# Experts by choice: five tiles ahead, late sums in a row, second weights behind the gates

## Chip, cores and metric

The kernel runs on one core of one Trainium2 chip. The metric is the device time of one execution in microseconds; before the change it is 3304.93 (median of 3 runs, 3302.91 to 3306.12).

## The reference, cut to what matters

The program is a graph attention layer with its own feed-forward part, followed by a layer of experts. Only the experts are touched:

```python
# x: 4096 tokens of 512 (normalized), 8 experts, hidden width 256, top 2
logits = xf @ router_w
gate_vals, idx = jax.lax.top_k(logits, K)
gates = jax.nn.softmax(gate_vals, axis=-1)
out = jnp.zeros_like(xf)
for e in range(E):
    h = jax.nn.relu(xf @ w1[e] + b1[e]) @ w2[e] + b2[e]
    y = _layernorm(xf + h, gamma[e], beta[e])
    w = jnp.sum(jnp.where(idx == e, gates, 0.0), axis=-1)
    out = out + w[:, None] * y
return out.reshape(B, S, D)
# and around it: x = x + experts(layernorm(x))
```

## The kernel before, in words

The stage `experts` (L1792) computes each token for its two chosen experts only. It has three phases.

Routing: the 32 tiles of 128 normalized tokens are loaded (L1948), transposed by PE and copied by ACT (`z_cols`), multiplied with the router, and DVE picks the best and the second-best expert per token. It computes the two gates of each token; ACT's queue stores them into the last two columns of the rows in HBM (`z3`, called `t_z` in the profile, L2049), 4096 pieces of 8 bytes. Semaphore `s_gate_home` tells of its landing.

Listing: DVE and PE sort the tokens by expert into slots of 128 tokens. `EACH = 39` slots hold the first choices (32 full tiles and up to 7 for the remainders of 8 experts), 39 more the second ones: 78 slots, each of one expert. The list of the first choices raises `s_ready` to 1 (L2212), the list of the second ones to 2.

Slots: for slot n, POOL gathers 128 rows by an indirect DMA into `rows_sb[n % 8]` (L1995). A row of a first choice comes from `z3` and has two halves: the row's running sum (514 numbers, `PART`), and the normalized row with its two gates. PE transposes (L2274), multiplies with the expert's w1 (`up`, L2332), transposes the hidden tile (L2340) and multiplies with w2 (`down`, L2351, with b2 in front, L2346). ACT copies the transposed rows (L2059), the hidden tile (L2064), applies relu and b1 (L2070), takes the root (L2099), and multiplies beta by the gate (`outer`, L2076). DVE adds down and rows (`y`, L2220), takes the statistics (L2222, L2224), adds the base (`add_base`, L2230), applies gamma (L2237) and adds up the slot before (`outer`, L2246), which raises `e_done`. Then POOL scatters: a first choice into `summed` (`t_summed`, whole rows, L2015), a second one into the output (L2012). A slot of the second choices reads its rows from `summed`, so all scatters of the first ones must have landed.

To let PE go on over that border, the first `LATE_PARTS = 5` slots of the second choices (39 to 43) are gathered in two pieces: the normalized half from `z3` early (L1989), the sum's half from `summed` late (`late_part`, L2003 to L2007, L2005 in the profile), with a semaphore for each (`moved_part`). DVE needs the late half in `add_base` only (L2228), and does that after `gain` in these slots. `all_put` (L1998) waits for the last four scatters of the first choices.

The order on each engine is written out by hand, and each queue is in order. POOL's loop (L2022) does, in iteration n, the gather of slot n + `LEAD`, then the scatter of slot n - 1 (which waits for `e_done`), then in iterations 39 to 43 the late part of slot n. A gather waits for its buffer: `e_done` of slot n - 8 and, for a first choice, the landing of its scatter (L1983 to L1985). PE's loop (L2363) does, in iteration n: the transpose of slot n + 2, up of n + 1, down of n, the transpose of the hidden tile of n + 1. ACT's loop (L2088) does the columns of n + 2, the hidden copies of n + 1, the root of n and outer of n + 1; ahead of the loop stands slot 0's outer, behind a wait for beta (L2085). DVE waits for gamma ahead of its first slot (L2250). PE waits for w1 ahead of the first up and for b2 and w2 ahead of its loop (L2361, L2362).

SP's queue (L1940) issues the weights after the last routing tile: b2's parts to HBM, b1, w1, w2, b2 back, gamma, beta. w1 and w2 have 4096 KB each, gamma and beta, copied to all partitions, 2048 KB each.

Of the kernel before, what the change touches and what calls it, by code (L numbers as in the profile page):

```python
# [10 lines left out]
P = 128  # L11
# [14 lines left out]
VROW = HEADS * VHEAD  # L26
PART = C + 2
WITH_SUM = 2 * PART
LATE_PARTS = 5
BOTH = C + VROW  # L30
MERGED = (3, 11, 19, 27)
DVE_HEADS = (HEADS - 1, HEADS - 2)
# [1759 lines left out]
def experts(nc, moved, moved_part, count, z3, router, w1, b1, w2, b2, gamma, beta, summed, b2_home, out):  # L1792
# [15 lines left out]
    EACH = T + E - 1  # L1808
    SLOTS = TOP * EACH
    TURN = 8  # L1810
    LEAD = 4
    Y = 4
    HALF = 4
    LIST_TURNS = 4
# [2 lines left out]
    with ExitStack() as ctx:  # L1817
        def sb(name, shape, dt=F32):
            return ctx.enter_context(nc.sbuf_tensor("m_" + name, shape, dt))

        def ps(name, shape, dt=F32):
            return ctx.enter_context(nc.psum_tensor("m_" + name, shape, dt))
# [3 lines left out]
        def sem(name):  # L1826
            used.append(ctx.enter_context(nc.semaphore("ms_" + name)))
            return used[-1]

        w1_sb, w2_sb = sb("w1", [P, E, KC, F]), sb("w2", [P, E, FC, C])  # L1830
# [48 lines left out]
        put_at = sb("put_at", [P, SLOTS], I32)  # L1879
        part_of = sb("part_of", [P, 2, LATE_PARTS], I32)  # L1880
        turned = [ps(f"turned{b}", [P, C]) for b in range(2)]
# [9 lines left out]
        s_w1, s_w2, s_b2, s_gamma, s_beta = (sem(n) for n in ("w1", "w2", "b2", "gamma", "beta"))  # L1891
        s_b2_rows, s_b2_cut, s_b2_home = sem("b2_rows"), sem("b2_cut"), sem("b2_home")
        s_c, s_cut, s_dve, s_low, s_ratio = (sem(n) for n in ("c", "cut", "dve", "low", "ratio"))
        s_counted, s_listed, s_ready, s_gate, s_gate_home = (sem(n) for n in ("counted", "listed_all", "ready", "gate", "gate_home"))
# [18 lines left out]
        def tile_rows(a, i, per, u):  # L1913
            v = a.rearrange("(n p) c -> n p c", p=P)
            return v[bass.ds(i * per + u, 1), :, :].rearrange("a p c -> (a p) c")
# [4 lines left out]
        def flat(x):  # L1920
            return x.rearrange("p a c -> p (a c)")

        def second(n):
            return n >= EACH

        def late(n):
            return EACH <= n < EACH + LATE_PARTS

# [3 lines left out]
        def wait_put(eng, n):  # L1932
            eng.wait_ge(put[n % Y], count + 16 * (n // Y + 1))
# [5 lines left out]
        @block.sync  # L1939
        def _(eng):  # L1940
            eng.dma_start(router_sb[:, :, :], router.rearrange("(k p) e -> p k e", p=P)).then_inc(s_c, 16)
            eng.dma_start(b2_rows[:, :], b2).then_inc(s_b2_rows, 16)
            z_of = z3[:, PART:PART + C]
            for i in range(T // TURN):
                for u in range(TURN):
                    if i:
                        r_turn.wait(eng, i - 1, u)
                    eng.dma_start(z_rows[:, u, :], tile_rows(z_of, i, TURN, u)).then_inc(r_load.sem(u), 16)  # L1948
            eng.wait_ge(s_b2_cut, 3 * PARTS - 4)
            eng.dma_start(b2_home, b2_parts[:, :, :]).then_inc(s_b2_home, 16)  # L1950
            eng.dma_start(b1_sb[:, :, :], b1).then_inc(s_w1, 16)
            eng.dma_start(w1_sb[:, :, :, :], w1.rearrange("e (k p) f -> p e k f", p=P)).then_inc(s_w1, 16)
            eng.dma_start(w2_sb[:, :, :, :], w2.rearrange("e (k p) c -> p e k c", p=P)).then_inc(s_w2, 16)
            eng.wait_ge(s_b2_home, 16)
            eng.dma_start(b2_sb[:, :, :], b2_home.rearrange("e k c -> k e c")).then_inc(s_b2, 16)
            for dst, a, landed in ((gamma_sb, gamma, s_gamma), (beta_sb, beta, s_beta)):
                eng.dma_start(flat(dst[:, :, :]), a.rearrange("e c -> (e c)").partition_broadcast(P)).then_inc(landed, 16)

        @block.gpsimd
        def _(eng):  # L1960
            for a, value in ((ones, 1.0), (zeros, 0.0), (eps, EPS), (ones_b, 1.0)):
                eng.memset(a[:, :], value).then_inc(s_cut, 1)
            eng.memset(go_on[:, :, :], 1.0).then_inc(s_cut, 1)
            eng.memset(go_on_e[:, :, :], 1.0).then_inc(s_cut, 1)
            for a, step, n, down, first_one in ((falling, -1, E, 0, E), (row_id, 0, 1, 1, 1), (slot_at, 1, EACH, 0, 0),
                                                (turn_b, 1, T, 0, 0)):
                eng.iota(a[:, :], pattern=[[step, n]], base=first_one, channel_multiplier=down,
                         allow_small_or_imprecise_dtypes=True).then_inc(s_cut, 1)
            eng.iota(iota_2[:, :, :], pattern=[[1, P], [0, 2]], base=0, channel_multiplier=0,
                     allow_small_or_imprecise_dtypes=True).then_inc(s_cut, 1)  # L1970
            eng.wait_ge(s_cut, 11)
            eng.memset(go_on[:, :, 0:1], 0.0).then_inc(s_cut, 1)
            eng.memset(go_on_e[:, :, 0:1], 0.0).then_inc(s_cut, 1)
            for m, of, op, other in ((ident, ones, ALU.is_equal, 0.0), (not_after, zeros, ALU.is_gt, -1.0)):
                eng.affine_select(out=m[:, :], in_=of[:, :], compare_op=op, fill=other, base=0,
                                  pattern=[[1, P]], channel_multiplier=-1).then_inc(s_cut, 1)

            z3_parts, summed_parts = (a.rearrange("n (h w) -> (n h) w", h=2) for a in (z3, summed))

            def gather(n):  # L1980
                u = n % TURN
                if n >= TURN:
                    e_done.wait(eng, 0, n - TURN)  # L1983
                    if not second(n - TURN):
                        wait_put(eng, n - TURN)  # L1985
                if late(n):
                    if n == EACH:
                        eng.wait_ge(s_ready, 2)
                    eng.indirect_dma_start(rows_sb[:, u, PART:], None, z3_parts,  # L1989
                                           bass.IndirectOffsetOnAxis(part_of[:, 1, n - EACH:n - EACH + 1], 0)  # L1990
                                           ).then_inc(got[u], 16)
                else:
                    if second(n):
                        all_put(n)
                    eng.indirect_dma_start(rows_sb[:, u, :], None, summed if second(n) else z3,  # L1995
                                           bass.IndirectOffsetOnAxis(row_of[:, n:n + 1], 0)).then_inc(got[u], 16)

            def all_put(n):  # L1998
                if n <= EACH + LATE_PARTS:
                    for k in range(EACH - Y, EACH):  # L2000
                        wait_put(eng, k)

            def late_part(n):  # L2003
                all_put(n)
                eng.indirect_dma_start(rows_sb[:, n % TURN, 0:PART], None, summed_parts,  # L2005
                                       bass.IndirectOffsetOnAxis(part_of[:, 0, n - EACH:n - EACH + 1], 0)
                                       ).then_inc(moved_part[n - EACH], 16)  # L2007

            def scatter(n):
                e_done.wait(eng, 0, n)  # L2010
                if second(n):
                    eng.indirect_dma_start(out, bass.IndirectOffsetOnAxis(put_at[:, n:n + 1], 0), y[:, n % Y, :], None,  # L2012
                                           bounds_check=NODES - 1, oob_is_err=False).then_inc(put[n % Y], 16)
                else:
                    eng.indirect_dma_start(summed, bass.IndirectOffsetOnAxis(put_at[:, n:n + 1], 0), rows_sb[:, n % TURN, :], None,  # L2015
                                           bounds_check=NODES - 1, oob_is_err=False).then_inc(put[n % Y], 16)

            eng.wait_ge(s_ready, 1)
            eng.wait_ge(s_gate_home, 16)
            for n in range(LEAD):  # L2020
                gather(n)
            for n in range(SLOTS):  # L2022
                if n + LEAD < SLOTS:
                    gather(n + LEAD)
                if n:
                    scatter(n - 1)
                if late(n):
                    late_part(n)
            scatter(SLOTS - 1)
            for n in range(SLOTS - Y, SLOTS):  # L2030
                wait_put(eng, n)
# [72 lines left out]
        def _(eng):  # L2104
# [69 lines left out]
            for c in range(TOP):  # L2174
# [33 lines left out]
                if c == 1:  # L2208
                    few = token[:, c, 0:LATE_PARTS]
                    st.link(nc.vector.tensor_scalar(part_of[:, 0, :], few, 2.0, None, ALU.mult))  # L2210
# [167 lines left out]
def graph_layer(nc, a, out):  # L2378
# [5 lines left out]
    with ExitStack() as ctx:  # L2384
        moved = [ctx.enter_context(nc.semaphore(f"moved{n}")) for n in range(MOVES)]
        moved_both = [ctx.enter_context(nc.semaphore(f"moved_both{n}")) for n in range(2)]
        moved_part = [ctx.enter_context(nc.semaphore(f"moved_part{n}")) for n in range(LATE_PARTS)]
        stages(nc, a, out, moved, moved_both, moved_part, scratch)
# [58 lines left out]
```

## Time and profile before

| | |
|---|---|
| median of 3 runs | 3304.93 us |
| profiled execution | 3307.92 us |
| its span | 3306.2 us |
| PE busy | 2772.7 us (84%) |
| DVE busy | 2521.6 us (76%) |
| ACT busy | 1701.4 us (51%) |
| POOL busy | 1935.0 us (59%) |
| routing, listing and slots | 2778 to 3306 us of the span |

The span runs from the first to the last instruction. Engines are PE (TensorE), DVE (VectorE), ACT (ScalarE), POOL (GpSimd) and SP; a q behind a name is its queue. A busy PE is not PE at its peak: the ends of matmuls are modelled, and a matmul that starts late can show as a longer one. Times of day below are microseconds from the start of the span.

### The profile page before, as it was taken

The page shows a single profiled execution, that of the slowest core. Times are in us where ns is not written, and L with a number is a line of the kernel's source. Part 1 is how long each engine was busy: PE and PEld are TensorE (multiplying, and loading weights), DVE is VectorE, ACT ScalarE, POOL GpSimd, SP SyncE. Part 2 cuts the span into 40 slices and gives each one's busy share as a digit, 9 for nine tenths or more (in the row PEclk, how much of TensorE's full clock was granted, in tenths as well). Part 3 has the DMA queues.
Part 4 walks back from the last instruction along what each step waited for, and adds up shares of the span by engine and source line. Part 5 has one row for each costly group of instructions (what it writes and reads, how often), then busy time and mean ns, then how long its engine had stood idle before and what let it go on. Part 6 is the DMA issues. An engine that isn't in the chain of part 4 may idle for free. (4 is left out here: it accounts for less than half of the span.)

```text
span 3306.2 us, 51862 instructions
## 1 busy us (share of the span) xinstructions
PE 2772.7 (84%) x12057; PEld 1710.6 (52%) x12057; DVE 2521.6 (76%) x5238; ACT 1701.4 (51%) x5713; POOL 1935.0 (59%) x1959
## 2 busy tenths in 40 slices
PE   6987888780888888886999999998999997699797
PEld 6544444450333333332555655567888885355454
DVE  8776666660999999998999999996566563577576
ACT  5222222220666566555999999993443432244343
POOL 2777777776777777776777777762222221044344
PEclk9888888885999999998999999997999999899999
DMA  4554555544888888887777878774221222765343
GB/s 168 197 182 167 173 173 170 174 147 152 261 258 261 262 260 259 261 258 243 216 231 231 233 231 232 230 205 112 68 71 61 74 71 94 226 200 188 119 155 108
DMA packets 248065, 610.11 MB, mean 185 GB/s; under 512 B 60466, under 2 KB 69578, under 8 KB 243037
## 3 DMA queue, kind: packets, MB, share of 16 engines
q0 software_dynamic: 130000, 376.49, 38.2%
q1 hardware_dynamic: 113661, 230.27, 20.2%
q8 instruction: 113, 1.85, 0.2%
q14 instruction: 179, 1.47, 0.1%
q10 hardware_dynamic: 4112, 0.03, 0.1%
HBM read 488.89 MB, written 123.26 MB: 185 GB/s over the span
## 5 line engine op out<-in xcount | busy, mean ns | idle before, releaser
L1275 PE MATMUL at_pair<-wide,hot_t 128*128 x1152 | 583.2, 621 | 120.7 <-ACT hot_t L1126 106.4
L1324 PE MATMUL at_pair<-product,v_hot 128*128 128x260 f32 x2304 | 617.2, 400 | 48.7 <-DVE product L1074 21.2
L364 POOL DMA_INDIRECT records<-staged,address x544 | 545.6, 1003 | 182.5 <-issue 161.9
L914 POOL DMA_INDIRECT fetched<-t_v,at_index x504 | 487.3, 967 | 188.0 <-issue 86.6
L904 POOL DMA_INDIRECT fetched<-t_k,at_index x504 | 487.4, 967 | 154.8 <-issue 102.0
L1324 PEld LDWEIGHTS at_pair<-product,v_hot 128*128 128x128 f32 x2304 | 394.5, 190 | 266.2 <-issue 158.4
L660 PE MATMUL qkv_prod<-wide 128*128 128x512 f32 x768 | 397.5, 681 | 96.8 <-ACT wide L404 96.8
L1066 DVE TENSOR_TENSOR wide<-at_pair,wide 128x520 f32 x576 | 397.3, 690 | 14.1 <-issue 10.3
L1275 PEld LDWEIGHTS at_pair<-wide,hot_t 128*128 128x128 f32 x1152 | 186.2, 189 | 385.0 <-issue 381.8
L1134 ACT ACTIVATE product<-product 128x64 f32<-128x64 f32 x864 | 215.9, 250 | 286.3 <-DVE product L993 284.9
L993 DVE TENSOR_TENSOR product<-at_pair,fetched 128x512 f32<-128x512 f32 x504 | 342.3, 682 | 25.3 <-DMA fetched<-t_k,at_index 18.9
L947 DVE TENSOR_REDUCE raw_score<-product 128x7 f32<-128x448 f32 x576 | 329.7, 575 | 0.0
L660 PEld LDWEIGHTS qkv_prod<-wide 128*128 128x128 f32 x768 | 165.6, 220 | 304.5 <-issue 205.6
L1213 ACT ACTIVATE product<-fetched,act_weight 128x65 f32<-128x65 f32 x1008 | 288.8, 333 | 0.0
L1074 DVE TENSOR_TENSOR product<-fetched,at_turn 128x390 f32<-128x390 f32 x504 | 276.4, 549 | 2.7 <-ACT act_weight L1193 1.5
L1526 POOL TENSOR_TENSOR f_base<-f_base,wide 128x512 f32<-128x512 f32 x32 | 41.0, 1280 | 343.6 <-DVE f_rows_in L1567 343.6
L1168 ACT ACTIVATE at_shared<-iota_f,low_neg 128x128 f32<-128x128 f32 x576 | 222.7, 387 | 0.0
L1718 PE MATMUL f_up<-f_zT,f_w 128*128 128x256 f32 x1536 | 192.5, 285 | 17.5 <-ACT f_h L1674 17.5
L1207 ACT ACTIVATE v_hot<-at_shared 128x128 f32<-128x128 f32 x576 | 175.8, 305 | 45.3 <-PE at_pair L1324 42.2
L1718 PEld LDWEIGHTS f_up<-f_zT,f_w 128*128 128x128 f32 x1536 | 186.7, 192 | 20.7 <-ACT f_h L1674 20.6
L1718 PE MATMUL f_down<-f_w,f_hT 128*128 128x512 f32 x768 | 185.6, 397 | 2.3 <-issue 2.3
L392 ACT COPY staged<-bias_sb 128x128 f32<-128x128 f32 x34 | 10.1, 297 | 333.2 <-DMA records<-staged,address 332.2
(327 smaller groups left out, 4647.7 us busy)
## 6 DMA issues: line engine op xcount, KB each, us to landing
row_bc<-in_src SPq DMA_DIRECT2D x34, 1024.0 KB, 5.4
pair_rows<-kept_v SPq DMA_DIRECT2D x72, 260.0 KB, 4.2
low_bc<-low_row SPq DMA_DIRECT2D x34, 512.0 KB
wide<-in_x SPq DMA_DIRECT2D x64, 256.0 KB, 3.2
t_z<-wide SPq DMA_DIRECT2D x64, 256.0 KB, 3.1
kept_v<-pair_rows SPq DMA_DIRECT2D x36, 260.0 KB, 3.7
kept_v<-at_shared SPq DMA_DIRECT2D x36, 260.0 KB, 3.8
records<-staged,address POOLq DMA_INDIRECT x544, 2.3
```

The costliest lines, as they stand in the source:

```text
L364: eng.indirect_dma_start(records, bass.IndirectOffsetOnAxis(address[:, b, u:u + 1], 0), staged[:, b, u, :], None,).then_inc(put[b][u], 16)
L660: last = nc.tensor.matmul(prod[n][:, :], zT[:, c, kc * P:(kc + 1) * P], w[:, n, kc, :], start=(kc == 0), stop=(kc == KC - 1))
L904: eng.indirect_dma_start(fetched[:, n % SLOTS, 0:C], None, k, bass.IndirectOffsetOnAxis(index[:, t:t + 1], 0)).then_inc(s_row[n % SLOTS], 16)
L914: eng.indirect_dma_start(fetched[:, n % SLOTS, :], None, v, bass.IndirectOffsetOnAxis(index[:, t:t + 1], 0)).then_inc(s_row[n % SLOTS], 16)
L947: nc.vector.tensor_reduce(raw[:, b, u % PAIR, u // PAIR, 0:heads], product[:, u % 4, 0:heads * D].rearrange("p (h d) -> p h d", d=D), AX.X ...
L993: nc.vector.tensor_tensor(product[:, u % 4, 0:C], q_edge[u % 4], key_rows(i, u), ALU.mult).then_inc(r_product.sem(u), 1)
L1066: nc.vector.tensor_tensor(to, pair[u % 3][:, :, 0:HALF], to, ALU.add).then_inc(r_total.sem(u), 1)
L1074: nc.vector.tensor_tensor(product[:, u % 4, 0:V_DVE * VHEAD].rearrange("p (h w) -> p h w", h=V_DVE), value_rows(m, u)[:, 0:V_DVE * VHEAD]. ...
L1213: ins = nc.scalar.activation(product[:, u % 4, h * VHEAD:(h + 1) * VHEAD], value_rows(m, u)[:, h * VHEAD:(h + 1) * VHEAD], ACT.Copy, scale ...
L1275: nc.tensor.matmul(q_edge[u % 4], hot_t[:, g % 2, u % BATCH * P:(u % BATCH + 1) * P], q_sb[:, bass.ds(at, 1), :].rearrange("p a c -> p (a ...
L1324: last = nc.tensor.matmul(pair[u % 3][:, n, 0:HALF], hot[:, u % 4, :], product[:, u % 4, n * HALF:(n + 1) * HALF], start=True, stop=True)
L1718: last = nc.tensor.matmul(out, stationary(a, k), moving(b, k), start=(k == 0 and n == 0), stop=(k == chunks - 1 and n == len(PASSES) - 1))
```

## The change

Two constants go up by one, the late parts are issued together, and two groups of loads change places around a new wait: SP waits for the landing of the gates, then issues b2, w2, gamma and beta in this order.

```diff
-LATE_PARTS = 5
+LATE_PARTS = 6
...
-    LEAD = 4
+    LEAD = 5
...
             eng.dma_start(w1_sb[:, :, :, :], w1.rearrange("e (k p) f -> p e k f", p=P)).then_inc(s_w1, 16)
-            eng.dma_start(w2_sb[:, :, :, :], w2.rearrange("e (k p) c -> p e k c", p=P)).then_inc(s_w2, 16)
+            eng.wait_ge(s_gate_home, 16)
             eng.wait_ge(s_b2_home, 16)
             eng.dma_start(b2_sb[:, :, :], b2_home.rearrange("e k c -> k e c")).then_inc(s_b2, 16)
+            eng.dma_start(w2_sb[:, :, :, :], w2.rearrange("e (k p) c -> p e k c", p=P)).then_inc(s_w2, 16)
             for dst, a, landed in ((gamma_sb, gamma, s_gamma), (beta_sb, beta, s_beta)):
                 eng.dma_start(flat(dst[:, :, :]), a.rearrange("e c -> (e c)").partition_broadcast(P)).then_inc(landed, 16)
...
                 if n:
                     scatter(n - 1)
-                if late(n):
-                    late_part(n)
+                if n == EACH:
+                    for m in range(LATE_PARTS):
+                        late_part(EACH + m)
             scatter(SLOTS - 1)
```

Slot 44 now belongs to those gathered in two pieces, and the six late parts all stand in POOL's queue behind the scatter of slot 38.

## Rows read from the trace of the kernel before

**Rows 1.** Busy time by stretch: engine us (instructions), granted clock, DMA share, GB/s.
```profile
2850.00:2900.00 50.00, 30.39 (x158) 19.97 (x158) 31.32 (x93) 16.71 (x37) 9.69 (x10) 0.71 0.58 182
2900.00:2950.00 50.00, 47.05 (x187) 28.75 (x188) 35.41 (x78) 22.48 (x59) 22.26 (x20) 1.00 0.61 202
...
3200.00:3250.00 50.00, 49.60 (x199) 30.25 (x198) 37.54 (x82) 23.37 (x62) 24.46 (x21) 1.00 0.47 154
```

**Rows 2.** Timeline of POOL: start, duration, instruction, idle before and its releaser.
```profile
2893.21 1.42 POOL L2015 DMA_INDIRECT t_summed<-m_rows,m_put_at  x1 [17.57 <-DVE m_rows L2246]
...
3086.73 1.01 POOL L2015 DMA_INDIRECT t_summed<-m_rows,m_put_at  x1 [1.93 <-DVE m_rows L2246]
...
3137.19 1.38 POOL L2012 DMA_INDIRECT out<-m_y,m_put_at  x1 [1.22 <-DVE m_y L2246]
...
3286.23 1.40 POOL L2012 DMA_INDIRECT out<-m_y,m_put_at  x1 [3.68 <-DVE m_y L2246]
...
3296.53 0.98 POOL L2012 DMA_INDIRECT out<-m_y,m_put_at  x1 [0.86 <-DVE m_y L2246]
```

**Rows 3.** The chain that ended last, in order of time: start, duration, what.
```profile
2849.19 18.43 DMA t_z<-m_gate
...
2890.70 0.70 DVE m_stats L2222
...
2894.93 5.38 DMA m_rows<-t_z,m_row_of
2901.57 1.99 PE m_up L2332 x8
...
2906.44 1.73 PE m_up L2332 x8
...
2911.06 1.73 PE m_up L2332 x8
```

**Rows 4.** Timeline at the border of the two halves, POOL, DVE and ACT.
```profile
3089.62 0.98 POOL L2005 DMA_INDIRECT m_rows<-t_summed,m_part_of  x1 [1.88 <-DMA t_summed<-m_rows,m_put_at]
...
3092.97 0.69 DVE L2230 TENSOR_TENSOR m_z_cols<-m_rows,m_z_cols 128x512 f32<-128x512 f32 x1 [6.26 <-DMA m_rows<-t_summed,m_part_of]
...
3095.50 0.29 ACT L2099 ACTIVATE m_root<-m_mv,m_eps 128x1 f32<-128x1 f32 x1 [6.50 <-DVE m_mv L2224]
```

**Rows 5.** DMA issues of the stage: size and median us to landing.
```profile
m_beta<-in_L_ffn_beta SPq DMA_DIRECT2D x1, 2048.0 KB, 19.9
...
t_summed<-m_rows,m_put_at POOLq DMA_INDIRECT x39, 3.8
```

**Rows 6.** Timeline of the first slots, all engines.
```profile
2889.97 0.69 DVE L2220 TENSOR_TENSOR m_y<-m_down,m_rows 128x512 f32<-128x512 f32 x1 [1.16 <-PE m_down L2351]
...
2908.95 0.37 ACT L2064 COPY m_h<-m_up 128x256 f32<-128x256 f32 x1
...
2910.24 0.38 PE L2340 MATMUL m_h_turned<-m_ident,m_h 128*128 128x128 f32 x2
```

**Rows 7.** DMA queues, 2850 to 2862 us: packets, MB, share of 16 engines.
```profile
q1 hardware_dynamic: 561, 4.69, 94.0%
q10 hardware_dynamic: 2187, 0.02, 11.3%
```

**Rows 8.** DMA queues, 2861 to 2862 us.
```profile
q10 hardware_dynamic: 1548, 0.01, 99.2%
```

**Rows 9.** Timeline at the start of the slots, all engines and queues.
```profile
2844.31 0.33 SPq L1957 DMA_DIRECT2D m_beta<-in_L_ffn_beta  x1
...
2861.03 0.20 DVE L2212 TENSOR_TENSOR m_put_at<-m_token,m_missing 128x39 int32<-128x39 f32 x1
...
2868.38 1.06 POOL L1995 DMA_INDIRECT m_rows<-t_z,m_row_of  x1 [85.92 <-DMA t_z<-m_gate]
...
2881.05 0.72 ACT L2076 ACTIVATE m_z_cols<-m_beta,m_rows 128x512 f32 x1
```

**Rows 10.** DMA queues, 2868 to 2882 us, the first six gathers alone.
```profile
q0 software_dynamic: 864, 3.16, 69.5%
```

## The prediction

> **What bounds the kernel now.** Only the last stage is touched, so I read it alone: first the busy time by stretch, then the POOL timeline (the pace of the slots), then the chain of waits (who sets that pace), then the start of the stage.
>
> The stage is a ring of 78 slots. In [rows 1] PE is busy 47 of 50 us in the first half and 49.6 of 50 in the second, but a slower form of the same matmuls hides waiting in that, so the pace has to come from the scatters. [Rows 2]: the scatter of slot 0 is issued at 2893.21 and that of slot 38 at 3086.73: 38 intervals in 193.5 us, 5.09 us each. From slot 38 to slot 44 (3137.19) it is 50.5 us for six. From slot 44 to slot 74 (3286.23) it is 149.0 us for 30, 4.97 each, and the last three take 10.3 us.
>
> [Rows 3] say what PE could do: one up starts at 2906.44 and the next at 2911.06, 4.62 us with nothing between but PE's own work. DVE isn't near: 37.5 of 50 us in [rows 1], about 3.7 us a slot. What breaks the 4.62 is the loop through the gather: PE's down ends, stats at 2890.70, outer, scatter at 2893.21, the gather behind it in POOL's queue at 2894.93, 5.38 us until it has landed, and PE goes on with up at 2901.57. From the down's end (about 2889.8) to landing are 10.5 us, to the next up 11.8. With four tiles ahead, gather m follows scatter m-6, which needs down m-5, and is wanted by the transpose after down m-3. So the loop is three slots of PE's order in 10.5 us plus what is left of one slot (4.6 us): 15.1 to 15.3 us, 5.0 to 5.1 us a slot. That is the measured 5.09, so the first half is bound by this loop. In the second half the gather is shorter and the pace 4.97 with some longer waits.
>
> The middle is bound otherwise: DVE waits 6.26 us for the late half of slot 39's rows, and ACT then 6.50 for DVE [rows 4]. Each late gather is queued behind a scatter, which waits for the slot before, which waited for its own late gather.
>
> **The change, part by part.** The sum is made against the profiled execution: span 3306.2 us, 1.7 us around it, 3307.9. The median of the timed runs, 3304.9, lies 3.0 lower; I subtract the difference from that.
>
> *Five ahead, first half.* Gather m now follows scatter m-7, so the loop gets four slots for the same 15.3 us: 3.8 us a slot, less than PE's 4.62. PE is next, and it is the bound. 38 x 4.62 = 175.6 against 193.5: **-17.9**. New behind the instruction: gather m waits for the scatter of m-8, now the last but one instead of the last but two. A scatter lands 3.8 us after issue [rows 5]; the next scatter is issued 4.62 after it and takes 1.4 plus 0.3, so the gather could start 6.3 us after it: covered, and a delay of 2 us more would cost nothing, as the gather has gained a slot. If the cover goes, scatter m-6 waits behind it (second rival). Bounds: 0 (nothing gained) and -17.9.
>
> *Late sums in a row.* The first late gather is where it was: slot 38's scatter must land (3086.73 to 3089.62 [rows 2, 4]), and DVE takes up its sum at 3092.97. Relative to an unbroken pace, DVE's y of slot 40 comes at 3093.7 instead of 3088.1, 5.6 late; ACT's root and the hidden copy behind it have 0.9 us of slack (the copy begun at 2908.95 takes 0.37, PE turns it at 2910.24 [rows 6]), so PE loses about **5**, once. The other five follow every 1.28 us (0.98 and 0.30) and have landed before DVE wants them, one per slot. The sixth replaces a whole gather, which is issued after all six at about 3097.3 on this clock and lands as slot 45 is wanted at about 3102: 0 to 1 us, taken in the 5. Bounds: the 5, and 22.7 as before (50.5 - 6 x 4.62).
>
> *Five ahead, second half.* 36 slots at 4.62, the last three in 10.3, plus the 5: 181.6, against 3296.53 - 3086.73 = 209.8: **-28.2**, of which 17.7 is the middle and 10.5 the pace. If the pace stays 4.97, the 10.5 is gone.
>
> *Loads moved behind the gates.* Before, the store of the gates (4096 pieces of 8 bytes, issued at 2849.19, landed 18.43 later [rows 3]) shares the engines with w2, gamma and beta. In 2850 to 2862 it got 2187 packets, 1548 of them in the last microsecond, when the loads ran out [rows 7, 8]. Alone it goes at 1550 a microsecond: 2.7 us of packets; from the end of the loads to landing it still took 6.6 us, since some engines lag, and with the first byte I take 8.5. It lands at about 2857.7 instead of 2867.6. The first gather then waits for the list (2861.03 plus 0.2 [rows 9]) and is issued at about 2862.0 instead of 2868.38: 6.4 us earlier.
>
> But SP now stands at the wait: the small b2 load, w2 (4.19 MB), gamma and beta (2.10 each), all behind it in SP's queue, start at 2858 instead of 2826 to 2844, and seven gathers (0.53 MB each, 3.7 MB) start at 2862 on the same engines. That is 12.1 MB. The loads before made 4.69 MB in 12 us, 391 GB/s [rows 7]: 31 us from 2860 (first byte), and 2 for the receipt (the beta load was issued at 2844.31 and took 19.9 to land, 2864.2, when the bytes ended about 2862 [rows 5, 9]). Beta is last: it lands at about 2893. Whoever shares first does not matter to that, only the bytes. Who waits: PE's down of slot 0 for w2 (about 2880, 4.19 MB shared), DVE's first spread for gamma, and ACT's first outer for beta, with slot 2's columns and slot 1's hidden copy behind it in ACT's queue. Before, this outer ran at 2881.05, nobody having waited for the load. After: outer at 2893, 0.71; columns 0.56; hidden 0.37; PE turns slot 1's hidden at 2895.0, and its down ends 4.6 later at 2899.6, against 2889.8 before (DVE's y of slot 1 at 2889.97 [rows 6]): +9.8. PE has stood still meanwhile. In 2850 to 2900 [rows 1] the granted clock was 0.71 on average, the 1.2 GHz level after PE had run out of work, so its first work comes at half speed: I add 2. **+12** in all, where the earlier gathers alone would give -6.4. Bounds: -6.4 (beta not late) and +18 (all 12.1 MB at the rate of gathers alone, 3.16 MB in 69.5% of 14 us or 325 GB/s [rows 10]: beta at 2860 + 37 + 2 = 2899).
>
> The Trainium skill speaks against this step ("DMA: Bandwidth & Descriptors", Rules for kernel authors: issue a DMA early, compute, wait late). Row and rule agree here that the early loads were hidden under the routing; by the rule the step would cost, as I take it. The same page (Where 436 GB/s comes from) puts the limit of loads from HBM at about 358 GB/s for a core; the trace shows 391 [rows 7], so the measurement decides. By 358, an estimate from the page, 12.1 MB would take 34 us and beta come 3 us later.
>
> *Nothing:* two longer instructions on six columns instead of five, one more semaphore.
>
> Sum: -17.9 - 28.2 + 12 = -34.1. Profiled execution 3273.8; median 3304.9 - 34.1 = **3270.8**.
>
> **The rivals.**
> - *The pace stops above 4.62*, say halfway, at 4.85 in the first half and 4.80 in the second. For it: the chain shows few waits of PE for a gather beside the many slots that are too long, so part may be PE's own reading of the expert's number behind the wait. Against: that reading is done in 4.62 too, wherever the rows had landed early, and PE's work is the same in both halves. First half -9.1; second 36 x 4.80 + 10.3 + 5 = 188.1, -21.7; with +12: -18.8, 3286.
> - *The scatter's landing takes the place of the gather's.* POOL is in order: the gather waits for the last scatter but one and holds the next scatter, so two slots take a landing plus 0.8 to wake and 1.3 for the gather. It decides from a landing of 2 x 4.62 - 2.1 = 7.1 us. With +12 at the start and -17.7 in the middle, 74 slots now at about 5.03 must be slower by 0.2 each to make the kernel slower by 9: pace 5.23, landing 8.4, over twice the 3.8 shown. 3314.
> - *The loads don't collide.* If gathers are let through and beta is in by 2881, the start is -6.4, the sum -52.5: 3252.4. For it: the engines were never full in the early gathers (325 of 391 GB/s). Against: the 12.1 MB have to pass.
> - *The change doesn't do what it says*: five ahead without a shorter loop (some other wait holds the gather). Both paces stay, only the middle gains: -17.7 + 12 = -5.7, 3299.
>
> **How the numbers follow.** Forecast 0.65; pace stops above 4.62: 0.15; loads don't collide: 0.09; no shorter loop: 0.07; slower: 0.04. A measurement here tells 0.2%, 6.6 us, from no change. Faster is the first three and 0.02 of the fourth, 0.91; same 0.05; slower 0.04. The forecast alone spans 3264 to 3277 (start +5 to +18). The range 3257 to 3290 takes in the slower pace and the middle between forecast and no collision.
>
> **What would show it.** Right: scatters of the first half every 4.62 us, PE waiting for no gather there; one DVE wait of about 6 us at slot 39 and none at 40 to 44; the gate's store landing near 2858; beta landing near 2893 on this clock, ACT idle before its first outer; scatter 0 at about 2905. Wrong: a POOL wait for a scatter's landing ahead of the gathers; ups that still start 4.8 to 5.1 us apart; an ACT that finds beta in place.

## The result

The changed kernel takes 3270.19 us (median of 4, 3270.01 to 3271.94) against 3305.52 for the kernel before on the same chip: ratio 0.9893, 95% interval 0.9876 to 0.991. The forecast was 3270.8 and the range held. In a second measurement it took 3274.82 against 3310.32: 0.9891 (0.9874 to 0.9907).

### The profile page after: what moved, and what is told of

It reads as the page before. It is cut to its first block and busy times, and to the rows that moved or that the text cites. A ratio compares the mean times of both kernels' runs of the same rounds, so it can differ in the third digit from the quotient of the medians.

```text
span 3268.5 us, 51867 instructions
## 1 busy us (share of the span) xinstructions
PE 2754.3 (84%) x12057; PEld 1708.9 (52%) x12057; DVE 2524.0 (77%) x5238; ACT 1701.4 (52%) x5713; POOL 1933.7 (59%) x1960
## 5 line engine op out<-in xcount | busy, mean ns | idle before, releaser
L1718 PE MATMUL f_up<-f_zT,f_w 128*128 128x256 f32 x1536 | 191.9, 285 | 18.1 <-ACT f_h L1674 18.1
```

The lines of the kernel that those rows point to most:

```text
L1718: last = nc.tensor.matmul(out, stationary(a, k), moving(b, k), start=(k == 0 and n == 0), stop=(k == chunks - 1 and n == len(PASSES) - 1))
```

## The profile after

The profiled execution takes 3270.25 us, its span is 3268.5. Line numbers behind L1956 are one or two higher than before. Where [rows 1] had 47 and 49.6 us of PE in 50, both halves are now full, and the border of the two halves shows as the only gap (same columns, kernel after):

```profile
2850.00:2900.00 50.00, 29.39 (x136) 19.32 (x137) 23.55 (x70) 14.01 (x29) 7.40 (x8) 0.67 0.63 243
2900.00:2950.00 50.00, 50.00 (x209) 31.54 (x208) 39.38 (x87) 24.73 (x66) 25.58 (x22) 1.00 0.66 217
...
3050.00:3100.00 50.00, 45.25 (x176) 28.14 (x174) 33.54 (x75) 21.14 (x56) 27.21 (x24) 0.93 0.48 141
3100.00:3150.00 50.00, 50.00 (x207) 31.50 (x207) 39.28 (x88) 24.48 (x65) 25.75 (x22) 1.00 0.53 168
```

The instruction counts say it without the modelled ends: 209 matmuls in 50 us where there were 187.

The start, in the chain of waits of the kernel after (start, duration, what). The gates' store takes 8.78 us and not 18.43 [rows 3]. Then beta's load is the chain, 28.89 us, and ACT's outer stands right behind it (at 2887.92, shown below):

```profile
2844.91 8.78 DMA t_z<-m_gate
...
2854.02 0.38 SPq L1956
...
2854.74 4.12 SPq L1958
...
2858.91 28.89 DMA m_beta<-in_L_ffn_beta
...
2889.44 0.44 PE m_h_turned L2342 x2
2889.88 0.81 PE m_turned L2276 x4
2890.69 3.07 PE m_up L2334 x8
```

The last row is an up that takes 3.07 us instead of 1.73. The timeline of the same stretch has the first gather (against [rows 9]: 19.19 us after the gates' store was issued, now 12.45, and its releaser is the list) and ACT's wait:

```profile
2857.36 1.01 POOL L1996 DMA_INDIRECT m_rows<-t_z,m_row_of  x1 [77.20 <-DVE m_put_at L2214]
...
2887.92 0.72 ACT L2078 ACTIVATE m_z_cols<-m_beta,m_rows 128x512 f32 x1 [14.42 <-DMA m_beta<-in_L_ffn_beta]
...
2899.34 1.42 POOL L2016 DMA_INDIRECT t_summed<-m_rows,m_put_at  x1 [33.41 <-DVE m_rows L2248]
```

The ring in its first half, POOL's timeline of the kernel after. Gathers stand 0.30 us behind the scatter, nothing holds them; a wait of 1.94 put down to the landing of an earlier scatter is as long as its neighbours put down to DVE, so that landing wasn't late:

```profile
2927.02 1.41 POOL L2016 DMA_INDIRECT t_summed<-m_rows,m_put_at  x1 [1.56 <-DVE m_rows L2248]
2928.73 0.97 POOL L1996 DMA_INDIRECT m_rows<-t_z,m_row_of  x1 [0.30 <-issue]
2931.64 1.44 POOL L2016 DMA_INDIRECT t_summed<-m_rows,m_put_at  x1 [1.94 <-DMA t_summed<-m_rows,m_put_at]
2933.38 0.97 POOL L1996 DMA_INDIRECT m_rows<-t_z,m_row_of  x1 [0.30 <-issue]
2936.25 1.40 POOL L2016 DMA_INDIRECT t_summed<-m_rows,m_put_at  x1 [1.91 <-DVE m_rows L2248]
```

And the border, all engines of the kernel after, against [rows 4]: DVE still waits 6.43 us for slot 39's late sum, but for no later one; PE stands 4.75 us for ACT's hidden copy and then does an up in 3.62 us that takes 1.89 otherwise:

```profile
3074.72 1.01 POOL L2016 DMA_INDIRECT t_summed<-m_rows,m_put_at  x1 [1.93 <-DVE m_rows L2248]
3077.63 0.98 POOL L2006 DMA_INDIRECT m_rows<-t_summed,m_part_of  x1 [1.90 <-DMA t_summed<-m_rows,m_put_at]
...
3081.13 0.69 DVE L2232 TENSOR_TENSOR m_z_cols<-m_rows,m_z_cols 128x512 f32<-128x512 f32 x1 [6.43 <-DMA m_rows<-t_summed,m_part_of]
...
3085.37 0.69 PE L2342 MATMUL m_h_turned<-m_ident,m_h 128*128 128x128 f32 x2 [4.75 <-ACT m_h L2066]
...
3086.70 3.62 PE L2334 MATMUL m_up<-m_w,m_zT 128*128 x8
...
3092.78 0.38 PE L2342 MATMUL m_h_turned<-m_ident,m_h 128*128 128x128 f32 x2
...
3093.44 1.89 PE L2334 MATMUL m_up<-m_w,m_zT 128*128 x8
```

## The yardstick of the experiments

All edits act behind one event, the issue of the gates' store, so every kernel is measured from there: to the first gather, to ACT's first outer, to scatter 0; then the scatters 0 to 38, 38 to 44, 44 to 74; and from the gates' store to the end of the span. These are differences of rows as in [rows 2], worked out for each kernel's one profiled execution (us). "Outer" is ACT's product of beta and gate, and the last columns are named by slots. Below, in brackets behind a time, stand its ratio to the kernel before and the 95% interval.

| kernel | gather 0 | outer 0 | scatter 0 | 0-38 | 38-44 | 44-74 | to the end |
|---|---|---|---|---|---|---|---|
| before | 19.2 | 31.9 | 44.0 | 193.5 | 50.5 | 149.0 | 457.0 |
| after | 12.5 | 43.0 | 54.4 | 175.4 | 35.4 | 138.4 | 423.6 |
| e1_loads_early | 19.3 | 32.0 | 44.2 | 175.4 | 35.0 | 138.5 | 413.1 |
| e2_loads_only | 12.3 | 40.5 | 52.9 | 194.3 | 51.5 | 147.9 | 466.5 |
| e3_ahead_only | 19.8 | 32.5 | 44.7 | 175.4 | 55.2 | 139.7 | 434.9 |
| e4_row_only | 19.5 | 32.5 | 44.7 | 189.7 | 38.9 | 147.9 | 441.3 |
| e5_six_ahead | 19.9 | 32.9 | 45.1 | 245.4 | 34.7 | 138.4 | 483.7 |
| e6_w2_early | 12.5 | 30.4 | 42.6 | 175.4 | 34.5 | 138.4 | 410.8 |
| e7_beta_behind | 15.5 | 29.9 | 42.1 | 175.4 | 34.4 | 138.4 | 410.2 |
| e8_base_later | 19.9 | 32.5 | 44.7 | 175.4 | 34.5 | 137.8 | 412.3 |
| e9_three_bases | 12.3 | 29.6 | 41.8 | 175.4 | 36.4 | 137.8 | 411.3 |
| e10_after_again | 12.5 | 41.5 | 53.7 | 175.4 | 34.2 | 138.4 | 421.7 |
| e11_gathers_between | 12.4 | 29.1 | 41.2 | 175.4 | 31.6 | 137.7 | 405.8 |

The last three slots take 10.3 us in all but e5 (10.5). In the first batch, e1 to e4, the unchanged stages ahead of the experts took some 650 us more in every kernel, the one before included (3948 us). Their mean granted clock was 0.85 to 0.86, where the other runs have 0.93; why is open. The lengths inside the experts' stage are the same as elsewhere (175.4 in e1 and e3), but the totals of that batch say little of one per cent.

## The experiments

**e1_loads_early.** The change without its moved loads:

```diff
-            eng.wait_ge(s_gate_home, 16)
+            eng.dma_start(w2_sb[...], w2...).then_inc(s_w2, 16)
             eng.wait_ge(s_b2_home, 16)
             eng.dma_start(b2_sb[...], b2_home...).then_inc(s_b2, 16)
-            eng.dma_start(w2_sb[...], w2...).then_inc(s_w2, 16)
```

> The changed kernel with the loads of w2, b2, gamma and beta put back where they were, without the wait for the gates. Theory (the moved loads cost the start: scatter 0 came 54.4 us after the gates' store was issued instead of 44.0): 10.4 less than the changed kernel, 3260; scatter 0 again 44 us after the gates' store, the pace still 4.62 in both halves. Rival A (the 4.3 us by which the gates' store came earlier on the clock is a gift of the moved w2, which no longer shares the engines with routing): only 6 less, 3264, with the gates' store at 2849 again. Rival B (the earlier gathers are needed for the pace): pace back above 4.62, 3275 or more.

Measured: 3905.13 against 3948.07 (0.9888, 0.9844 to 0.9931). Scatter 0 comes at 44.2 and not at 54.4, the pace stays, and 413.1 us from the gates' store to the end are 10.5 less than the changed kernel's. The moved loads cost what they were said to cost, and the pace doesn't need them. Rival A isn't decided here: the gates' store is issued 70.9 us after the stage began, against 70.8 before the change and 68.8 with it; e10 takes this up.

**e2_loads_only.** The kernel before with the moved loads alone (the diff's SP part).

> The kernel before with nothing but the moved loads. Theory: the start costs 10.4, 3316, the rest as before (38 intervals at 5.09, 50 us in the middle). Rival A: 3312, with the gates' store 4 us earlier on the clock. Rival (the loads don't collide, the earlier gather is a gain): 3299.

3957.94 against 3948.07 (1.0035, 1.0005 to 1.0066): slower. Scatter 0 at 52.9, 8.9 later, and 466.5 to the end, 9.5 more. ACT's outer, which waits for beta, comes 2.5 us earlier than in the changed kernel. Of that, 1.0 is the gates' store, which landed after 7.8 us instead of 8.8; the other 1.5 is about what one gather of 0.53 MB takes at 391 GB/s (1.4, an estimate), and with four tiles ahead there are six gathers beside beta and not seven.

**e3_ahead_only.** Five ahead, the late parts one by one, loads early:

```diff
-                if n == EACH:
-                    for m in range(LATE_PARTS):
-                        late_part(EACH + m)
+                if late(n):
+                    late_part(n)
```

> The kernel before with five tiles ahead and six slots in two pieces (the fifth tile ahead needs the sixth), but each late part behind its own scatter as before, and the loads early. Theory: first half 18.1 less, second half's pace 10.6 less, and one more serial late part, 4.3 more: 3281; scatters 38 to 44 some 54 us apart. Rival (the loop through the gather isn't what bounds, the row of late sums does it): pace 5.09, 3306 to 3310.

3930.72 against 3948.07 (0.9966, 0.994 to 0.9993). 175.4 us for the first half, as with the whole change; 55.2 at the border, 4.7 more than before; 139.7 behind it. The pace is the doing of the fifth tile (with the sixth slot in two pieces that it needs), without the row of late sums and without the moved loads.

**e4_row_only.** The same edit the other way round, on the kernel before (`LEAD` 4, five late parts in a row).

> The kernel before with its five late parts issued in a row behind the scatter of slot 38, four tiles ahead, loads early. Theory: only the middle gains, 15 to 18: 3288 to 3291, pace 5.09 and 4.97 as before. Rival (the late sums are bound by DVE or by the engines' bandwidth, not by POOL's order): at most 5 less, 3300.

3942.36 against 3948.07 (0.9974, 0.9949 to 1.0). The border takes 38.9 instead of 50.5, 11.6 less, short of the 15 to 18. The chain of waits of e4_row_only names the rest. With four ahead the whole gather of slot 44 stands behind the five late parts and PE waits for it, then works at a granted clock of 0.50:

```profile
3743.25 0.94 POOL m_rows L2005
3744.49 5.27 DMA m_rows<-t_summed,m_row_of
3749.81 1.11 PE m_turned L2275 x4
3750.92 2.96 PE m_up L2333 x8
```

So the sixth slot in two pieces is more than the price of the fifth tile: with it the next whole gather is slot 45's, one slot later. The first half's 189.7 is 3.8 under the kernel before without a cause in the edit (194.3 in e2). I take it that this loop's pace follows the gathers' landing from run to run; that isn't shown.

**e5_six_ahead.** As e1, `LEAD = 6`, `LATE_PARTS = 7`.

> As e1_loads_early, with six tiles ahead and seven slots in two pieces. Theory (POOL's gather waits for the landing of the scatter of the tile that had its buffer, and holds the next scatter): that scatter is now the one issued just before, so each slot of the first half takes a landing of 3.7 plus 0.8 to wake and 1.3 for the gather, 5.8 us; scatters 0 to 38 some 220 us apart instead of 175; the second half, which has no such wait, stays at 4.62. Rival (a deeper lead only adds slack): 175 us as in e1_loads_early.

3333.39 against 3311.64, one run each; to the end 483.7 us against 457.0, so the stage is slower than before the change. 245.4 us for 38 slots, 6.46 each; the second half unchanged. The prediction's second rival, the one that ended on the slower side, is a real mechanism, one tile further on. POOL's timeline of e5_six_ahead shows it: scatter, then 4.1 us of waiting until that tile's scatter has landed, gather, and the next scatter only behind it.

```profile
2958.65 0.97 POOL L1995 DMA_INDIRECT m_rows<-t_z,m_row_of  x1 [4.10 <-DVE m_rows L2247]
2959.92 1.01 POOL L2015 DMA_INDIRECT t_summed<-m_rows,m_put_at  x1 [0.30 <-issue]
2965.03 1.40 POOL L1995 DMA_INDIRECT m_rows<-t_z,m_row_of  x1 [4.10 <-DMA t_summed<-m_rows,m_put_at]
2966.74 1.02 POOL L2015 DMA_INDIRECT t_summed<-m_rows,m_put_at  x1 [0.30 <-issue]
```

From scatter to gather are 5.1 us where I had 4.5, so the cycle is 6.4 and not 5.8.

**e6_w2_early.** The changed kernel, w2 and b2 early again, gamma and beta behind the gates:

```diff
-            eng.wait_ge(s_gate_home, 16)
+            eng.dma_start(w2_sb[...], w2...).then_inc(s_w2, 16)
             eng.wait_ge(s_b2_home, 16)
             eng.dma_start(b2_sb[...], b2_home...).then_inc(s_b2, 16)
-            eng.dma_start(w2_sb[...], w2...).then_inc(s_w2, 16)
+            eng.wait_ge(s_gate_home, 16)
```

> The changed kernel with w2 and b2 early again, only gamma and beta behind the gates. Theory (beta's landing is set by the bytes that must pass after the gates: now 4.2 MB of loads and 3.7 of gathers at 390 GB/s): gates land 9 us after their store is issued, beta about 33 after it instead of 42.9, scatter 0 at about 44 instead of 54.4, no gain over all loads early (44.2). Rival (w2 itself is what PE waits for, beta follows at once): scatter 0 at 40 or less.

The gates land after 9.7 us. Beta lands 23.7 us after their store was issued and not 33, and ACT's outer at 30.4 doesn't wait for it any more, so the sum by bytes fails here. The loads pass ahead of the gathers, as the DMA view of e6_w2_early from 2858 to 2872 us has it (queues as in [rows 7], issues as in [rows 5]):

```profile
q1 hardware_dynamic: 288, 4.19, 71.0%
q0 software_dynamic: 288, 1.09, 19.1%
...
m_beta<-in_L_ffn_beta SPq DMA_DIRECT2D x1, 2048.0 KB, 13.3
m_rows<-t_z,m_row_of POOLq DMA_INDIRECT x7, 12.2
```

Both loads are through, and of the seven gathers' 3.7 MB only 1.09 have moved. What now comes last is the first gather. It is issued 6.8 us earlier than in e1, but PE's first transpose (2872.10) comes only 1.8 us earlier, 24.0 us after the gates' store instead of 25.8. In e9, which has the same loads, the chain of waits names this gather, with 10.42 us where it took 5.17 before the change:

```profile
2859.36 10.42 DMA m_rows<-t_z,m_row_of
```

Scatter 0 comes at 42.6, 1.6 better than with all loads early, where no gain was expected; e9 and e11 have 41.8 and 41.2 with these loads, against 44.0 to 45.1 in the six profiles with all loads early. The whole took 3260.59 in one run.

**e7_beta_behind.** As e6, the wait in front of beta's load only.

> As before, but only beta waits for the gates; w2, b2 and gamma early. Theory: three early loads are through 6 us after the gates' store is issued, so the gates land 13 to 15 after it instead of 18.5, the first gather comes at 14 to 15, and beta shares with the gathers alone: scatter 0 between 40 and 44. Rival (the gates are starved as before): first gather at 19, beta late behind it, scatter 0 at 46 or more.

The gates land after 14.7, the first gather comes at 15.5, scatter 0 at 42.1: inside the expectation. The chain of waits of e7_beta_behind now runs through the first gather, which shares the engines with beta's load:

```profile
2871.43 7.56 DMA m_rows<-t_z,m_row_of
```

It took 5.01 us in e1, so 2.5 of the 3.8 us won at its issue are lost there. Beta is in 22.1 us after the gates' store was issued, and ACT's outer at 29.9 doesn't wait for it. 3266.28 in one run; to the end 410.2, as e6.

**e8_base_later.** As e1; DVE's order in the slots in two pieces:

```diff
                 if n:
+                    if late(n - 1):
+                        add_base(n - 1)
                     outer(n - 1)
                 if not late(n):
                     add_base(n)
                 gain(n, e)
-                if late(n):
-                    add_base(n)
```

> As e1_loads_early; in the slots in two pieces DVE adds the base after the next slot's statistics instead of before them. Theory (PE stands 4.75 us because ACT's hidden copy waits for DVE's statistics of slot 40, held by slot 39's late sum, and then starts at half clock): scatters 38 to 44 some 30 us apart instead of 35.0, no half-speed up behind. Rival (DVE has too much to do there whatever the order): 34 to 36.

3260.84 in one run. The border takes 34.5, not 30: the rival's number, by another cause. DVE's statistics of slot 40 were in time, but ACT's outer of slot 41 waits for the base buffer that slot 39's late sum still holds, and the hidden copy stands behind it. PE stands 2.82 us instead of 4.72 (e1), and its clock falls all the same: the up behind takes 2.79 us instead of 1.89. The timeline of e8_base_later, ACT and PE:

```profile
3074.08 0.72 ACT L2077 ACTIVATE m_z_cols<-m_beta,m_rows 128x512 f32 x1 [3.73 <-DVE m_z_cols L2231]
...
3075.18 0.38 ACT L2065 COPY m_h<-m_up 128x256 f32<-128x256 f32 x1
...
3075.61 0.69 PE L2341 MATMUL m_h_turned<-m_ident,m_h 128*128 128x128 f32 x2 [2.82 <-ACT m_h L2065]
...
3076.94 2.79 PE L2333 MATMUL m_up<-m_w,m_zT 128*128 x8
```

**e9_three_bases.** As e6, with e8's order and a third base buffer:

```diff
-        base = spare[:, 2 * C:4 * C].rearrange("p (n c) -> p n c", c=C)
+        base = spare[:, 2 * C:5 * C].rearrange("p (n c) -> p n c", c=C)
...
-                e_base.wait(eng, 0, n - 2)
+                e_base.wait(eng, 0, n - 3)
```

In the two instructions that write and read this buffer, `base[:, n % 2, :]` becomes `base[:, n % 3, :]`.

> As e6_w2_early (gamma and beta behind the gates), with the base added after the next slot's statistics as in e8_base_later, and three buffers for the product of beta and gate instead of two. Theory (in e8_base_later ACT's outer of slot 41 waited 3.7 us for the base buffer that slot 39's late sum still held, so PE stood all the same): with the third buffer DVE's statistics of slot 41 come 2.7 us late instead of ACT's of slot 40 5.6, PE loses about 2 and no clock: scatters 38 to 44 some 30 us apart instead of 34.5, from the gates' store to the end 406 us, 17 less than the changed kernel (423.6). Rival (something else holds PE at the border): 34 again, 411 us.

3263.4 against 3310.32 (0.986, 0.9843 to 0.9876). The border takes 36.4, worse than the 34.5 of e6 and e8. PE stands 1.73 us for the hidden copy, as forecast, but being earlier it now outruns slot 45's gather, which six late parts have pushed back in POOL's queue. In the timeline of e9_three_bases, POOL and PE:

```profile
3072.63 0.95 POOL L2006 DMA_INDIRECT m_rows<-t_summed,m_part_of  x1 [0.30 <-issue]
...
3073.88 0.94 POOL L1996 DMA_INDIRECT m_rows<-t_summed,m_row_of  x1 [0.30 <-issue]
...
3075.11 0.44 PE L2342 MATMUL m_h_turned<-m_ident,m_h 128*128 128x128 f32 x2 [1.73 <-ACT m_h L2066]
...
3078.71 1.11 PE L2276 MATMUL m_turned<-m_ident,m_rows 128*128 128x128 f32 x4 [3.16 <-DMA m_rows<-t_summed,m_row_of]
...
3079.62 3.73 PE L2334 MATMUL m_up<-m_w,m_zT 128*128 x8
```

**e10_after_again.** The changed kernel beside e9.

> The changed kernel as it is, beside e9_three_bases on the same chip, for the comparison of the two. Theory: from the gates' store to the end 423.6 us as before, 0.989 of the kernel before; the 4.3 us by which the gates' store came earlier on the clock in its first profile are not the change's (routing took 68.8 to 71.2 us in the runs so far, with no order by where the loads stand), and the stage begins when the unchanged stages let it. Rival (they are the moved loads'): routing at 68.8 again.

3274.82 against 3310.32 (0.9891). To the end 421.7, 1.9 less than in the first profile: scatter 0 comes 0.7 earlier, and the border is 1.2 shorter. PE stands for the same 4.75 us there, but its clock comes back sooner, and the up takes 2.82 us instead of 3.62. From this transpose of the hidden tile to the next are 6.23 us, in the first profile 7.41 (3085.37 to 3092.78), where an undisturbed slot has 4.62. PE's timeline of e10_after_again:

```profile
3089.07 0.69 PE L2342 MATMUL m_h_turned<-m_ident,m_h 128*128 128x128 f32 x2 [4.75 <-ACT m_h L2066]
...
3090.41 2.82 PE L2334 MATMUL m_up<-m_w,m_zT 128*128 x8
...
3095.30 0.38 PE L2342 MATMUL m_h_turned<-m_ident,m_h 128*128 128x128 f32 x2
```

The gates' store is issued at 2849.32, as late as before the change, so the 4.3 us as a whole were not the change's. Routing, from the start of the stage to that issue, took 68.8 us again; but e5, with its loads early, took 68.7, and e2, with its loads moved, 70.6. The rival isn't borne out, nor is it excluded: both profiles of the changed kernel have 68.8, and the other five with all loads early have 70.8 to 71.2. These 2 us stay unexplained.

**e11_gathers_between.** As e9, POOL's order at the border:

```diff
-                if n + LEAD < SLOTS:
+                if n + LEAD < SLOTS and n not in (EACH + 1, EACH + 2):
                     gather(n + LEAD)
...
                     for m in range(LATE_PARTS):
                         late_part(EACH + m)
+                        if m in (1, 2):
+                            gather(EACH + LATE_PARTS + m - 1)
```

> As e9_three_bases, with the whole gathers of slots 45 and 46 put between the late parts (after the second and the third) instead of behind all six and behind scatter 39. Theory (in e9_three_bases PE stood 3.16 us for slot 45's gather, which six late parts had pushed back in POOL's queue, and then worked at half clock): gather 45 is issued 5 us earlier and lands before PE wants it; what is left is some 2 us at slot 41: scatters 38 to 44 some 30 us apart instead of 36.4, 405 us from the gates' store to the end. Rival (the late sums, pushed back in their turn, stop DVE instead): 34 or more.

3255.44 against 3305.75: 0.9851 (0.9837 to 0.9865), the fastest of all; its 405.8 us to the end are 17.8 less than the changed kernel's in its first profile, 15.9 less than in its second. The border takes 31.6, 4.8 less than in e9, and PE's clock stays up: in the 50 us around the border (same columns as [rows 1], kernel e11_gathers_between) it is 1.00 where the changed kernel had 0.93. The expected 30 is missed by 1.6; the rival's 34 isn't reached.

```profile
3050.00:3100.00 50.00, 47.78 (x195) 29.26 (x194) 36.99 (x81) 22.73 (x60) 28.62 (x27) 1.00 0.50 158
```

## Why the prediction was right, step by step

The mechanism was right in all three parts; what the sum left out is the half-speed work at the border. That the total was hit within a microsecond is luck: the terms are right to within 3 us each, and the profiles differ by 4 ahead of the stretch that the forecast dealt with. Between the two profiled executions the difference is 3307.9 - 3270.2 = 37.7 = 18.1 + 25.7 - 10.4 + 4.3, the last of it ahead of the gates' store; whether 2 of these 4.3 are the moved loads' stays open (e10).

- **The loop through the gather, first half** (-17.9): -18.1. Shown by e3, where the fifth tile alone does it, and by e2 and e4, which keep four tiles ahead and have 5.11 and 4.99 a slot. Before the change the slots weren't even: POOL's timeline has many of 4.62 us and between them some of 5.2 to 6.7, and it is their mean, three slots in 15.3 us, that fits the loop. PE's own 4.62 is next: 175.4 in all nine profiles with five ahead.
- **The second half's pace** (-10.5): -10.6. e3, with the fifth tile alone, takes 139.7 for these 30 slots where the whole change takes 138.4; e2 and e4, with four tiles ahead, take 147.9. The rival that the pace stops above 4.62 is refuted.
- **The gather's wait for a scatter's landing** cost nothing with five ahead, and e5 shows where it would have: with six the gather waits for the scatter just issued, and a slot takes 6.46 us.
- **The border** (-17.7): -15.0. The PE wait was right (5 said, 4.75 measured), its reason too. The mis-sized term is PE's clock: I priced the half-speed restart at the start of the slots but not here. The slot behind the wait takes 7.41 us from transpose to transpose instead of 4.62, 2.8 more, which is the 2.7 missing. It is no fixed price: in e10, behind the same wait, it was 1.6, and the border 1.2 us shorter.
- **The gates' store alone** (8.5 us, landing): 8.8, and 7.4 to 9.7 in the others that hold gamma and beta back.
- **The moved loads** (+12): +10.4, and +9.7 in the repeat, +8.9 in e2. Beta was expected 43.8 us after the gates' store and landed at 42.9. From ACT's outer to PE's transpose it took 0.5 less than I had. The 2 for the half-speed work came out: from that transpose (2889.44) to the down's end (2895.99) are 6.55 us where I had 4.6 at full speed. So 9.8 + 2 - 0.9 - 0.5 gives the 10.4. The rival that the loads don't collide is refuted by e1 and e2 together. One step of this term holds less widely than I wrote it, that only the bytes matter and not who shares first. It held where w2, gamma, beta and seven gathers passed together; with w2 out of the way (e6) the same sum gave 33 us, and beta landed at 23.7, ahead of the gathers. The Trainium skill says to issue a DMA early and to wait for it late ("DMA: Bandwidth & Descriptors", Rules for kernel authors). The runs agree for the step as a whole, which cost 10.5 us (e1), and not for its smaller form with w2 early, which gained 1.6 at scatter 0 (e6).

The first gather is issued 6.7 us earlier, and beta then costs that and 10.4 more. With gamma and beta alone behind the gates (e6), the first gather is as early, but it then takes some 5 us longer beside these loads, and 1.6 us are left at scatter 0.

## What to carry to other kernels

Before adding a tile of lead, write down for each instruction in the queue which event it waits for and how many slots back that is: one more tile took a whole loop off the path, two more put another one on it. When a load is held back for the sake of a small transfer, everything behind it in the queue is held back with it; sum the bytes that must then pass together with what starts at that moment, hold back only what is needed last, and look at both sides afterwards: at the load, and at the small transfers that now share the engines with it. A stall of PE, where it is the bound engine, costs its length and then the half-speed work behind it: 4.75 and 2.8 us here, 4.75 and 1.6 in the repeat.

## What the runs showed of the hardware

- Under 391 GB/s of loads the store of 4096 pieces of 8 bytes hardly moved (639 packets in 11 us, from [rows 7, 8]); with gamma and beta held back, or w2 too, it landed in 7.4 to 9.7 us (six profiles).
- PE's clock fell to the lower level (granted 0.50) while PE stood for 4.75 us in the kernel after, and while it stood for 2.82 us in e8; the ups behind took 3.62 and 2.79 us instead of 1.89. In e9 it held through a wait of 1.73 us and fell in the next one of 3.16, little later (up 3.73). In e11 it held through a wait of 1.67 (granted clock 1.00, up 1.99).
- The time at the lower level isn't set by the wait alone: behind 4.75 us of standing the up took 3.62 us in one profile of the changed kernel and 2.82 in the other (e10).
- Loads and gathers don't always share alike: with two loads (e6, 2858 to 2872 us) 4.19 MB of loads passed beside 1.09 of gathers, with three (kernel after, below) 3.30 beside 2.11.
- Loads and gathers together passed at the rate of loads alone (391 GB/s [rows 7]): kernel after, DMA queues from 2856 to 2870 us (packets, MB, share of 16 engines), 5.41 MB in 14 us, 386 GB/s.

```profile
q1 hardware_dynamic: 1613, 3.30, 62.2%
q0 software_dynamic: 572, 2.11, 38.3%
```
